# A two-layer vision tower with a mixture of experts: routing chosen from unscaled logits, counts summed on TensorE, gate weights formed at the experts, and another order of row transfers and row turns

## What is computed

```python
scores = jax.nn.softmax(x @ wg, axis=-1)
gates, idx = jax.lax.top_k(scores, k)                       # k = 2, E = 8, N = 2048
gates = gates / jnp.clip(jnp.sum(gates, -1, keepdims=True), EPS)
masks = jax.nn.one_hot(idx, E, dtype=jnp.int32)
counts = masks.sum(0)
offsets = jnp.concatenate([jnp.zeros((1, E), jnp.int32), jnp.cumsum(counts, 0)[:-1]], 0)
loc = jnp.cumsum(masks, 0) - 1 + offsets[None]
loc_sel = (loc * masks).sum(-1)
keep = loc_sel < C                                          # C = 640
pos = jnp.where(keep, idx * C + loc_sel, E * C)
buf = jnp.zeros((E * C + 1, D), x.dtype).at[pos.reshape(-1)].set(xk)
h = jax.nn.silu(jnp.einsum('ecd,ehd->ech', disp, fc1_w) + fc1_b[:, None, :])
y = jnp.einsum('ech,ehd->ecd', h, fc2_w) + fc2_b[:, None, :]
combined = jnp.sum(gates[..., None] * ybuf[pos], axis=1)
```

## Time and profile before

| | |
|---|---|
| median of 3 runs | 999.82 us (998.98 to 1000.0) |
| profiled execution | 999.01 us, span 997.1 us |
| TensorE products | 855.4 us busy (86%), x4842 |
| TensorE weight loads | 541.8 us (54%), x4842 |
| VectorE | 542.0 us (54%), x2095 |
| ScalarE | 421.5 us (42%), x741 |
| GpSimd | 304.6 us (31%), x365 |
| mean granted TensorE clock | 0.922 |

### The profile page before, as it was taken

How to read it: one execution, slowest core, us unless ns; L and a number is a source line. 1 busy time by engine, 2 the same in 40 slices (tenths; PEclk the granted TensorE clock), 3 DMA queues, 4 the chain that set the end, 5 groups by cost and what they waited for, 6 DMA issues and landing times. The chain is left out here.

```text
span 997.1 us, 14099 instructions
## 1 busy us (share of the span) xinstructions
PE 855.4 (86%) x4842; PEld 541.8 (54%) x4842; DVE 542.0 (54%) x2095; ACT 421.5 (42%) x741; POOL 304.6 (31%) x365
## 2 busy tenths in 40 slices
PE   6979999898898899899889798349999999999940
PEld 2655556545455455355445243236877877877830
DVE  1268535779798799799878777410211211210136
ACT  1315434587585586686455556113021021022005
POOL 6113223434334333222253423460203212302332
PEclk9998999999799799899799689669999999999975
DMA  9652211202202202201321301631145135233242
GB/s 345 207 188 65 59 29 48 81 1 66 65 2 65 65 1 65 66 23 44 86 84 43 106 7 61 223 116 43 16 127 143 22 122 143 27 120 71 27 110 84
DMA packets 57510, 81.48 MB, mean 82 GB/s; under 512 B 6624, under 2 KB 51041, under 8 KB 55008
## 3 DMA queue, kind: packets, MB, share of 16 engines
q1 hardware_dynamic: 49520, 70.48, 22.0%
q0 software_dynamic: 7296, 9.47, 5.7%
q10 hardware_dynamic: 624, 0.63, 0.2%
HBM read 35.37 MB, written 19.68 MB: 55 GB/s over the span
## 5 line engine op out<-in xcount | busy, mean ns | idle before, releaser
L1102 DVE CUSTOM_DVE_ANT_0 junk<-ps,maskb 128x256 bf16<-128x256 f32 (+4 forms) x512 | 205.8, 434 | 66.3 <-PE ps L821 64.9
L647 ACT ACTIVATE probs<-ps 128x512 f32<-128x512 f32 (+1 forms) x304 | 157.4, 552 | 95.6 <-PE ps L844 91.3
L1559 PE MATMUL ps<-dxT,qs 128*128 128x320 f32 x512 | 141.1, 436 | 1.3 <-DVE dxT L1633 1.3
L1571 PE MATMUL ps<-ks,hTe 128*128 128x256 f32 x640 | 139.3, 379 | 0.0
L1593 ACT ACTIVATE hTe<-ps,qs 128x640 f32<-128x640 f32 x64 | 50.8, 793 | 204.6 <-PE ps L1559 204.6
L1515 POOL DMA_INDIRECT mixed_rows<-ysb,ids x40 | 61.7, 1543 | 228.1 <-DVE ysb L1653 225.2
L1571 PEld LDWEIGHTS ps<-ks,hTe 128*128 128x128 f32 x640 | 121.1, 190 | 16.3
L1559 PEld LDWEIGHTS ps<-dxT,qs 128*128 128x128 f32 x512 | 97.9, 192 | 42.5 <-DVE dxT L1633 1.9
L844 PE MATMUL ps<-qs,ks 99*128 99x256 bf16 (+4 forms) x512 | 107.7, 296 | 15.3 <-DVE nmax L1102 9.0
L821 PE MATMUL ps<-ks,qs 96*128 96x256 bf16 (+4 forms) x512 | 108.8, 299 | 12.6 <-DVE nmax L1102 7.3
L860 PE MATMUL ps<-probs,vaug 128*32 128x256 f32 (+4 forms) x1024 | 92.6, 437 | 6.2 <-POOL probs L557 5.6
(11 more groups left out here) (188 smaller groups left out, 1193.0 us busy)
## 6 DMA issues: line engine op xcount, KB each, us to landing
qs<-parts SPq DMA_DIRECT2D x96, 128.0 KB, 2.4
ks<-parts SPq DMA_DIRECT2D x96, 128.0 KB, 2.4
qs<-w SPq DMA_DIRECT2D x8, 1024.0 KB, 9.5
ks<-w SPq DMA_DIRECT2D x8, 1024.0 KB, 4.9
dispatched_rows<-att SPq DMA_DIRECT2D x8, 650.0 KB, 10.4
ks<-dispatched_rows SPq DMA_DIRECT2D x4, 650.0 KB, 7.2
x_sb<-xT SPq DMA_DIRECT2D x8, 256.0 KB, 3.9
mixed_rows<-h SPq DMA_DIRECT2D x4, 512.0 KB, 3.3
```

The costliest lines, as they stand in the source:

```text
L647: act.activation(probs_of(u)[:, heads[0]:heads[-1] + 1, :], turned_bank((u, half, i))[:, 0:len(heads) * w].rearrange("p (j n) -> p j n", n=w),
L1102: ins = dve.tensor_tensor_reduce(out=junk[:, b - (b > V_BANK), a * (hi - lo):(a + 1) * (hi - lo)], in0=score_bank((u, half, i))[:, a * (hi ...
L1559: ins = mm(bank(2 * (n % 2) + c)[:, 0:HC], w1s[:, e % 2, k, m * P:(m + 1) * P], dxT[:, e % 2, k, c * HC:(c + 1) * HC], start=(k == 0), sto ...
L1571: ins = mm(bank(4 + n % 2)[:, 0:D], hTe[:, e % 2, m, t * P:(t + 1) * P], w2s[:, e % 2, m, :], start=(m == 0), stop=(m == MH - 1))
```

## The change

Routing. The root of the layer norm's variance no longer scales the logits ahead of the choice, since a positive factor changes no order: VectorE chooses both experts from `cur`, the logits less the mean's part. The exponents' scaling goes to GpSimd (two operations over nine columns, step 2), two exponentials to ScalarE (step 3). The sum of a token's exponentials, the second expert's exponential and a mark of the first expert go into the row's spare columns, and `meta` forms the weights from them at the experts. The counting products move to step 4, and one wider product and four that repeat a tile's counts replace two, so that the sums over tiles come out of TensorE. Positions come in steps 5 and 6 with the expert's offset already in `base`. Phase "route" has 7 steps in place of 10.

Order. A send issues one transfer in a half step and has eight; send 2 starts at 268 in place of 271. For the last batch GpSimd normalises the four tiles in place of VectorE. The wait for all transfers and the first row loads move behind the barrier. TensorE runs 20 products of 512 columns (`WARM`) before it turns rows; nothing reads what they write. Expert 1's tiles are turned within the first product of expert 0, and those of expert e+2 one by one within the second product of expert e.

The diff, cut; lines that it takes from `route`, `turn_rows` and `evac_rows` stand in the code above and are left out here, and each piece is moved to the left:

```diff
+WARM_SENDS, WARM = 5, 20
...
-    ("o", 6, 245), ("gate", 2, 258), ("route", 2, 260), ("send", 2, 271), ("o", 7, 278), ("gate", 3, 282),
+    ("o", 6, 245), ("gate", 2, 258), ("route", 2, 260), ("send", 2, 268), ("o", 7, 278), ("gate", 3, 282),
     ("route", 3, 284), ("send", 3, 293),)
-STEPS = {"tok": 12, "qkv": 8, "o": 7, "ffn": 28, "gate": 2, "route": 10, "send": 4, "bias": 2, "wq": 4}
+STEPS = {"tok": 12, "qkv": 8, "o": 7, "ffn": 28, "gate": 2, "route": 7, "send": 8, "bias": 2, "wq": 4}
...
-return ("cnt",) if c == 6 else ()
+return ("cnt",) if c == 4 else ()
...
-sp.wait_ge(scattered, 16 * 2 * NTT)
-load_rows(sp, 0)
-load_rows(sp, 1)
...
                         if phase == "send":
-                            t = c
-                            if t == 0:
+                            t, k = divmod(c, 2)
+                            if c == 0:
                                 pool.wait_ge(routed, i + 1)
+                                pool.wait_ge(ln_done, NORMED["o", B + i] + NT)
                                 pool.wait_ge(zeroed, 16 * (E + 1))
                                 if i:
                                     pool.wait_ge(scattered, 16 * 2 * NT * i)
-                            for k in range(2):
-                                pool.indirect_dma_start(
-                                    out=disp, out_offset=bass.IndirectOffsetOnAxis(ap=posu[:, i, t, k:k + 1], axis=0),
-                                    in_=h3[:, i * NT + t, :], in_offset=None, bounds_check=ROWS - 1,
-                                    oob_is_err=False).then_inc(scattered, 16)
+                            pool.indirect_dma_start(
+                                out=disp, out_offset=bass.IndirectOffsetOnAxis(ap=posu[:, i, t, k:k + 1], axis=0),
+                                in_=h3[:, i * NT + t, :], in_offset=None, bounds_check=ROWS - 1,
+                                oob_is_err=False).then_inc(scattered, 16)
                         if phase == "o" and c == 4:
                             roots(0, NT, ROOTS["o", i])
+                        if phase == "o" and i == 2 * B - 1 and c == 5:
+                            pool.wait_ge(rstd_done, ROOTS["o", i])
+                            for t in range(NT):
+                                pool.tensor_scalar(h3[:, (B - 1) * NT + t, 0:D], att[:, i % 2, t, :], mv[:, t, 0:1],
+                                                   rstd[:, t:t + 1], ALU.subtract, ALU.mult).then_inc(ln_done, 1)
+                        if phase == "route" and c == 2:
+                            def wide(v):
+                                return v.rearrange("p (t o) -> p t o", o=1).to_broadcast([P, NT, E + 1])
+                            pool.wait_ge(lowered, i + 1)
+                            pool.wait_ge(rstd_done, ROOTS["o", B + i])
+                            pool.tensor_tensor(exps_of[:, :, :], low[:, :, :], wide(mx[:, :]),
+                                               ALU.subtract).then_inc(low_chain, 1)
+                            pool.wait_ge(low_chain, i + 1)
+                            pool.tensor_tensor(exps_of[:, :, :], exps_of[:, :, :], wide(rstd[:, :]),
+                                               ALU.mult).then_inc(scaled, 1)
...
-if phase == "route" and c == 0:
-    act.wait_ge(lowered, i + 1)
-    act.activation(pp[:, 0, :, :], rt[:, :, :], ACT.Exp).then_inc(raised, 1)
+if phase == "route" and c == 3:
+    act.wait_ge(scaled, i + 1)
+    act.activation(h3[:, i * NT:(i + 1) * NT, D + 2], exps_of[:, :, E], ACT.Exp)
+    act.activation(pp[:, 0, :, :], exps_of[:, :, 0:E], ACT.Exp).then_inc(raised, 1)
...
-if phase == "route" and c == 6:
+if phase == "route" and c == 4:
     pe.wait_ge(chosen, i + 1)
     o = d_open(("route", i, "cnt"))
-    mf = mk[:, :, :, :].rearrange("p t a b -> p (t a b)")
-    mm(o[:, 0:2 * E * NT], trib[:, 0:P], mf, start=True, stop=True)
-    mm(o[:, 2 * E * NT:4 * E * NT], trib[:, P:2 * P], mf, start=True,
-       stop=True).then_inc(d_full(("route", i, "cnt"))[0], 1)
+    w = 2 * E
+    mm(o[:, 0:w * (NT + 1)], trib[:, 0:P], mk[:, :, :, :].rearrange("p t a b -> p (t a b)"),
+       start=True, stop=False, skip_group_check=True)
+    for t in range(NT):
+        ins = mm(o[:, w * (t + 1):w * (NT + 1)].rearrange("p (n k) -> p n k", k=w),
+                 trib[:, P:2 * P], mk[:, t:t + 1, :, :].rearrange("p t a b -> p t (a b)")
+                 .to_broadcast([P, NT - t, w]), start=False, stop=(t == NT - 1),
+                 skip_group_check=True)
+    ins.then_inc(d_full(("route", i, "cnt"))[0], 1)
...
     dve.wait_ge(*d_out(("gate", i, "lg")))
+    then(dve.tensor_reduce(mx[:, :], cur, AX.X, ALU.max))
+    then(dve.tensor_tensor(rt[:, :, :], cur, wide(mx[:, :]), ALU.is_equal))
 if c == 1:
+    then(dve.tensor_tensor(rt[:, :, :], rt[:, :, :], rev, ALU.mult))
+    then(dve.tensor_reduce(tiles[:, :, D + 3], rt[:, :, :], AX.X, ALU.max))
+    then(dve.tensor_tensor(mk[:, 0:NT, 0, :], rt[:, :, :], wide(tiles[:, :, D + 3]),
+                           ALU.is_equal))
+    then(dve.scalar_tensor_tensor(pp[:, 1, :, :], mk[:, 0:NT, 0, :], MASKED, cur, ALU.mult,
+                                  ALU.add))
+    dve.tensor_reduce(low[:, :, E], pp[:, 1, :, :], AX.X, ALU.max).then_inc(lowered, 1)
+    dve.wait_ge(lowered, i + 1)
+if c == 2:
+    then(dve.tensor_tensor(rt[:, :, :], pp[:, 1, :, :], wide(low[:, :, E]), ALU.is_equal))
+    then(dve.tensor_tensor(rt[:, :, :], rt[:, :, :], rev, ALU.mult))
+    then(dve.tensor_reduce(rc[:, :], rt[:, :, :], AX.X, ALU.max))
+    dve.tensor_tensor(mk[:, 0:NT, 1, :], rt[:, :, :], wide(rc[:, :]),
+                      ALU.is_equal).then_inc(chosen, 1)
+if c == 5:
     dve.wait_ge(raised, i + 1)
+    link(5, dve.tensor_reduce(tiles[:, :, D + 1], pp[:, 0, :, :], AX.X, ALU.add))
     dve.wait_ge(*d_full(cnt))
+    v = dense_bank(cnt)
+    old, new = base[:, i % 2, :, :], base[:, (i + 1) % 2, :, :]
+    link(5, dve.tensor_tensor(
+        sel[:, :, 0:2, :], v[:, 0:2 * E * NT].rearrange("p (t k e) -> p t k e", t=NT, e=E),
+        old.rearrange("p (o k) e -> p o k e", o=1).to_broadcast([P, NT, 2, E]), ALU.add))
+    dve.tensor_tensor(new, old, v[:, 2 * E * NT:2 * E * (NT + 1)].rearrange(
+        "p (k e) -> p k e", e=E), ALU.add).then_inc(d_out(cnt)[0], 1)
     dve.wait_ge(*d_out(cnt))
+    linked(5)
+    then(dve.tensor_tensor(sel[:, :, 2, :], sel[:, :, 1, :], new[:, 0:1, :].to_broadcast(
+        [P, NT, E]), ALU.add))
+if c == 6:
+    link(5, dve.scalar_tensor_tensor(
+        sel[:, :, 1, :], sel[:, :, 1, :], -1.0,
+        per_expert(2).rearrange("p (o e) -> p o e", o=1).to_broadcast([P, NT, E]), ALU.mult,
+        ALU.add))
+    then(dve.tensor_tensor(past[:, :, :, :], sel[:, :, 0:3:2, :], per_expert(1).rearrange(
+        "p (o k e) -> p o k e", o=1, k=1).to_broadcast([P, NT, 2, E]), ALU.is_ge))
+    then(dve.scalar_tensor_tensor(past[:, :, :, :], past[:, :, :, :], 2.0 * ROWS,
+                                  sel[:, :, 0:2, :], ALU.mult, ALU.add))
+    then(dve.tensor_tensor(past[:, :, :, :], past[:, :, :, :], mk[:, 0:NT, :, :], ALU.mult))
+    then(dve.tensor_reduce(loc[:, :, :], past[:, :, :, :], AX.X, ALU.add))
+    dve.tensor_copy(posu[:, i, :, :], loc[:, :, :]).then_inc(routed, 1)
...
-if c in (5, 6):
+if c in (5, 6) and i < 2 * B - 1:
...
+sp.wait_ge(scattered, 16 * 2 * NTT)
+load_rows(sp, 0)
+load_rows(sp, 1)
 for e in range(E - 2):
     sp.wait_ge(xT_done, CT * (e + 1))
-    if e == 0:
-        sp.wait_ge(gate_chain, 1)
+    sp.wait_ge(gate_chain, 2 * e + 1)
...
+def turn_rows(e, t):
+    n = e * CT + t
+    if e == 0:
+        pe.wait_ge(first_in[t], 16)
+    elif t == 0:
         pe.wait_ge(rows_in[e % 2], 16 * (e // 2 + e % 2))
...
 n = e * MH + m
+if e == 0 and m >= MH - CT:
+    turn_rows(1, m - (MH - CT))
...
 n = e * CT + t
+if e + 2 < E:
+    turn_rows(e + 2, t)
...
-turn_rows(0)
+pe.wait_ge(scattered, 16 * (2 * NTT - WARM_SENDS))
+for _ in range(WARM):
+    mm(bank(0), identb[:, :], qgu[:, 0, 0:S], start=True, stop=True)
+for t in range(CT):
+    turn_rows(0, t)
 fc1(0)
-turn_rows(1)
 for e in range(E):
     if e + 1 < E:
         fc1(e + 1)
-    if e + 2 < E:
-        turn_rows(e + 2)
     fc2(e)
...
     dve.tensor_copy(ids[:, e, :], m[:, :, D]).then_inc(ids_done, 1)
+    then(dve.tensor_scalar(gw[:, 0, :], m[:, :, D + 1], 1.0, None, ALU.max))
+    then(dve.reciprocal(gw[:, 0, :], gw[:, 0, :]))
+    then(dve.tensor_tensor(gw[:, 1, :], m[:, :, D + 2], gw[:, 0, :], ALU.mult))
+    then(dve.tensor_tensor(gw[:, 2, :], gw[:, 0, :], gw[:, 1, :], ALU.add))
+    then(dve.tensor_scalar(gw[:, 2, :], gw[:, 2, :], EPS_GATE, None, ALU.max))
+    then(dve.reciprocal(gw[:, 2, :], gw[:, 2, :]))
+    dve.tensor_tensor(gw[:, 0, :], gw[:, 0, :], gw[:, 2, :], ALU.mult)
+    then(dve.tensor_tensor(gw[:, 1, :], gw[:, 1, :], gw[:, 2, :], ALU.mult))
+    dve.scalar_tensor_tensor(gts[:, e, 0, :], m[:, :, D + 3], float(E - e), gw[:, 0, :],
                              ALU.is_equal, ALU.mult)
```

(21 more changed lines are left out.)

134 lines of the change are left out of this document (34 added, 100 removed).

## The result

The changed kernel takes 973.64 us (median of 4; 972.26 to 975.11) against 999.4 us before (4; 996.51 to 1000.0): a ratio of 0.9746, 95% interval 0.9724 to 0.9769. It is faster by 25.8 us; I had said 980.5 with a range of 972 to 989, which holds it, and 974 to 987 for the likeliest case alone, which misses it by 0.4. The profiled execution took 975.11 us with a span of 973.0, 24.1 us less than the span before, and its mean granted clock is 0.935 (0.922 before).

The account below looks back on a forecast made before the run. It saw late GpSimd masks and low clock in attention, one chain at its end, then TensorE alone as bounds. Gains 5.0 + 3.0 + 4.5 + 1.8 + 4.8 = 19.1 us gave 980.5 us, range 972 to 989.

Parts of the forecast that it names:

- the likeliest case: Whole kernel: the summed forecast of 980.5 us holds, chance 0.60, with its own range of 974 to 987 us.
- with a part of the low clock staying: Batch 1's two later attention windows: 29.4 us now, at least 23.5 after, taken as 24.9, so 4.5 us gained.
- its named waits are 3.2 us: Batch 0's routing in attention: no free window compares, so named waits of 1.8 + 1.4 us give a 3.0 us gain.
- The terms 5.0 and 3.0: Routing during attention: gains of 5.0 us for batch 1 (bounds 1 and 8) and 3.0 for batch 0 (0 and 6).
- More than the sum: Rival, chance 0.10: all low clock in attention goes and turns cost 1.04 us, giving 971 us.
- End of attention, 4.5 us: Batches 2 and 3: mask 2.3 us later, root at once, first transfer at 640.9 against 645.74; 4.5 us gained (2 to 6).
- Hand-over, 1.8 us: From last transfer to the experts: third stage at X + 28.7 instead of X + 30.5; 1.8 us gained (0 to 4.4).
- the loads are issued as before, 1.45 us after: Handing over to the experts: row loads still issued 1.45 us after the last transfer.
- follows GpSimd by about 0.4 us: Handing over to the experts: the barrier, which waited for the load issue, now follows GpSimd by about 0.4 us.
- X: Handing over to the experts: end of the last transfer's issue, 655.71 before; turns forecast at X + 7.3 against X + 4.6.
- Experts, 4.8 us: Turns within products cost 1.4 us an expert (bounds 1.04 and 2.20); six experts gain 4.8 us (0 to 7).
- Slower: Rival, chance 0.03: semaphore pauses before every tile lower TensorE's clock; two experts' worth would give 1030 us.

Follow-up runs that it names:

- the row loads ahead of the barrier: Changed kernel without the 20 products before the turns and with the first row loads back ahead of the barrier: 973.03 us, ratio 0.9733.
- the combination with 24: Changed kernel, third batch's transfers from half step 271, two normalising passes on VectorE, 24 filler products beside the last transfers, 8 behind the barrier: 963.16 us.
- The fill: Changed kernel with ten products of 512 columns in front of TensorE's wait for GpSimd's last mask: 973.17 us, ratio 0.9733.
- the order with the mask first: Changed kernel with the third batch's transfers from half step 271, behind GpSimd's last mask, in place of 268: 970.81 us, ratio 0.9721.
- the packed kernel: Changed kernel with two transfers in each of 4 half steps, the third batch's from half step 271: 980.27 us, ratio 0.9804.
- the combinations: Changed kernel, transfers from 271, shared normalising, 8 fillers behind the barrier and 24, 44 or 38 in the first block: 963.16, 969.1, 964.46 us.

## Why the forecast was right, and where it was not

**Attention, the step "with a part of the low clock staying" and "its named waits are 3.2 us".** The direction held: spacing and fewer operations both pay. The terms 5.0 and 3.0 were mis-sized; they measured 9.6 and 8.9. Three steps failed. For batch 1 I added GpSimd's 12.9 us to a free block and called 23.5 us the least; the 12.9 came, across both blocks, and these took 21.1. I priced VectorE's 19 operations at their own 4.0 us; given back in four half steps they cost 5.8 to 6.4, and TensorE's named waits, which rose by 3.0 and 3.7 us, are only a part of that. The rest goes with a lower clock; that the waits lower it in these blocks was my reading, and no run shows it; *Open* has blocks with a low clock and fewer waits. For batch 0 I took only named waits, though two of the three blocks of the earlier trace rows had a clock of 0.77 and 0.83. And 2.9 of batch 0's 8.9 us may be luck of the profile: in two others with the same attention (*the row loads ahead of the barrier*, and the combination with 24) its three blocks took 45.4 us, a gain of 6.0. My case *More than the sum* had the low clock going, at a chance of 0.10 and with 3 us a batch where 4.6 and 5.9 more came.

**End of attention, 4.5 us.** Every stall went where I said: the mask 2.5 us late (2.3 foreseen), the root at once. Two prices failed. I let the late mask cost its own time and no more; the 2.60 us that TensorE waited for it also put the next 11.33 us at 0.70, 2.1 us more. The fill and the order with the mask first both show it, and so do all profiles: with the mask late and nothing in TensorE's wait the stretch took 10.9 to 11.8 us in six, with the mask in time 9.2 in six and 10.45 in one, at a clock of 0.84 that nothing here explains. And a normalising pass cost 1.21 us, not 0.5. My bounds, 0.35 and 0.72, came from a VectorE row and a two-input row of GpSimd; the pass with two per-partition operands lies outside both. I had written that 1.3 us a pass would cost 2.4 us; 1.21 cost 1.7. The rest of the chain was right: with two passes on VectorE it took 8.12 us from the last variances to the first transfer, 8.1 by the forecast. The Trainium skill, GPSIMD Engine Reference, section 3.1, from which I had an estimate of 0.56 us, is measured there on a plain addition; the measurement here is twice that and decides.

**Hand-over, 1.8 us.** The step "the loads are issued as before, 1.45 us after" misread the diff: it moves them behind the barrier. And "follows GpSimd by about 0.4 us" failed: I took the barrier's 0.4 us behind SyncE's last issue for its price behind GpSimd. It opens 3.0 to 3.2 us after GpSimd's last transfer issue in all ten profiles with the loads behind it and nothing else holding it. So turns began at X + 9.2, not X + 7.3, though the 20 products took 5.77 us and not my 6.9. That the products pay was wrong too in this place (0.9 us lost); begun while the transfers are issued they do pay.

**Experts, 4.8 us.** Right mechanism: 1.09 us an expert, where I took 1.4 between 1.04 and 2.20. 1.11 x 6 = 6.7 of the 6.9 measured. In the case *Slower* the sum is off: two experts at double length add 69.6 us, which gives 1050 us and not 1030.

That the sum, 19.1 for 24.1, was no worse is luck, for the errors cancel: 10.5 more from attention and 2.1 more from the experts met 3.8 and 2.2 less from the two steps between, and 1.5 less from stretches that I held for unchanged.

**Open.** Batch 0's first two blocks, with the same instructions, took 27.7 us at 1.00 in eight profiles and 30.7 at 0.78 and 0.89 in two (and in the packed kernel), though TensorE's named waits there are shorter in one of the two (1.0 us in the combination with 24) than in the changed kernel (1.9). No run here says what sets it. The Trainium skill, TensorE: Matmul & The Clock Gate, Part 1, says that the length of the slow phase at a kernel's start varies from run to run of one kernel. These blocks stand in the middle of different kernels, so no run here shows that case, but they vary in the same way. Nor is it known why an engine sometimes begins 1 to 3 us late at the end of attention; the DMA engines were full then (share 1.01).

## What to carry to other kernels

Price a wait of TensorE twice: its own length and the clock of what follows. In a block whose granted clock is low, the named waits are not the whole loss. Put DMA issues of a slow queue one at a time between the work that others wait for, never ahead of the last piece on which the chain hangs. Filler products paid here where they ran beside the transfers and ended against the real work; begun behind the barrier they cost more than they brought.

## What the runs showed of the hardware

- 2.6 us without work on TensorE was followed by 11.3 us at a mean clock of 0.70; with 2.11 us of it filled, the stretch behind ran at 1.00.
- Behind 17.3 us without products, 20 products of 512 columns took 5.77 us at a mean clock of 0.74, and 6.54 in the kernel with the mask first. In the combinations eight products behind 4.9 us of nothing took 3.57 us (clock 0.50), behind 0.9 us of nothing 1.89.
- A GpSimd pass over 128x256 float32 with two per-partition operands took 1.21 to 1.29 us, VectorE's 0.35 to 0.41. A two-input pass of GpSimd over 36 columns took 0.24.
- The barrier opened 3.0 to 3.2 us after GpSimd's last indirect transfer issue, and, where SyncE's loads stood ahead of it, 0.4 us after the last of them.
